# Expert stage: hots and masks in PSUM ring A, half 1's choice earlier in each engine's order, two bias rows issued as a couple

## The reference, cut to what matters

```python
xf = layernorm(x)                              # 1024 x 512
logits = xf @ router_w                         # 1024 x 8
gate_vals, idx = top_k(logits, 2)
gates = softmax(gate_vals)
for e in range(8):
    h = relu(xf @ w1[e] + b1[e]) @ w2[e] + b2[e]
    y = layernorm(xf + h, gamma[e], beta[e])
    out = out + sum(where(idx == e, gates, 0))[:, None] * y
x = x + out
```

## Time and profile before

| | us |
|---|---|
| median of 3 runs | 1158.26 |
| the 3 runs | 1157.27, 1158.26, 1162.53 |
| the profiled execution | 1157.11 |
| its span, first to last instruction | 1155.3 |

### The profile page before, as it was taken

One profiled execution on the slowest core, in us unless ns is written; L12 is line 12 of the kernel. 1 busy time (PEld: TensorE's weight loads), 2 busy tenths in 40 slices (PEclk: granted clock), 3 DMA queues, 4 the chain that ended last, 5 costly groups with the idle time before them and its releaser, 6 DMA issues.

```text
span 1155.3 us, 16126 instructions
## 1 busy us (share of the span) xinstructions
PE 1083.4 (94%) x5992; PEld 881.8 (76%) x5992; DVE 707.9 (61%) x1530; ACT 366.2 (32%) x671; POOL 149.1 (13%) x141
## 2 busy tenths in 40 slices
PE   3999799999999999999898999999999999999986
PEld 2777699888777777776898977777778888777653
DVE  7576777479676567457665479764653117723667
ACT  4234466525321211136566325221300011001132
POOL 4230202000000000300202000000000705000036
PEclk8999999999999999999999999999999999999897
DMA  6230101002312112000101004211337201100001
GB/s 210 84 117 1 38 2 38 1 5 92 90 48 64 56 47 78 1 1 1 38 1 38 1 5 130 72 46 55 108 148 246 74 1 37 35 1 1 1 18 55
DMA packets 34654, 60.16 MB, mean 52 GB/s; under 512 B 19440, under 2 KB 20400, under 8 KB 33936
## 3 DMA queue, kind: packets, MB, share of 16 engines
q1 hardware_dynamic: 12688, 41.21, 10.9%
q10 hardware_dynamic: 21888, 17.87, 4.8%
HBM read 48.59 MB, written 10.49 MB: 51 GB/s over the span
## 4 chain that ended last, share of the span: by engine, by line
PE 79%; DVE 11%; ACT 4%; issue 4%; POOL 1%; DMA 0%; ACTq 0%; POOLq 0%; DVEq 0%
PE ps_a L528 10%; PE ps_a L530 10%; PE ps_a L529 10%; PE ps_v L528 10%; PE ps_v L529 9%; PE ps_v L530 9%; PE ps_a L885 5%; PE ps_v L725 4%; PE ps_v L736 3%; PE ps_a L549 2%; PE ps_a L660 2%; DVE expk L1532 2%; ACT work L1063 1%; DVE qmax L1626 1%; PE ps_v L614 1%
## 5 line engine op out<-in xcount | busy, mean ns | idle before, releaser
L528 PE MATMUL ps_a<-ht_hi,w_hi 128*128 128x512 f32 x488 | 193.8, 397 | 2.7 <-DVE w_lo L1798 0.9
L530 PE MATMUL ps_a<-ht_hi,w_lo 128*128 128x512 f32 x488 | 191.6, 393 | 0.0
L529 PE MATMUL ps_a<-ht_lo,w_hi 128*128 128x512 f32 x488 | 191.3, 392 | 0.0
L974 ACT ACTIVATE work<-ps_a,col_sb 128x512 f32<-128x512 f32 x96 | 66.7, 719 | 203.0 <-PE ps_a L530 144.7
L528 PEld LDWEIGHTS ps_a<-ht_hi,w_hi 128*128 128x128 f32 x488 | 92.5, 189 | 26.0 <-DVE headmask_r L1497 1.3
L1651 DVE TENSOR_TENSOR xm<-ps_v,xm 128x512 f32<-128x512 f32 x80 | 55.2, 690 | 86.0 <-PE ps_v L530 85.5
L530 PEld LDWEIGHTS ps_a<-ht_hi,w_lo 128*128 128x128 f32 x488 | 92.3, 189 | 19.9
L529 PEld LDWEIGHTS ps_a<-ht_lo,w_hi 128*128 128x128 f32 x488 | 92.4, 189 | 19.4
L528 PE MATMUL ps_v<-w_hi,f_hi 128*128 128x512 f32 x256 | 101.7, 397 | 0.0
L528 PE MATMUL ps_v<-w_hi,ht_hi 128*128 128x512 f32 x224 | 92.0, 411 | 9.7 <-issue 5.8
L530 PE MATMUL ps_v<-w_hi,f_lo 128*128 128x512 f32 x256 | 99.7, 389 | 0.0
(11 more groups left out here) (238 smaller groups left out, 1964.9 us busy)
## 6 DMA issues: line engine op xcount, KB each, us to landing
stage<-wstream SPq DMA_DIRECT2D x62, 512.0 KB, 3.7
adj_d<-adj_win ACTq DMA_DIRECT2D x16, 256.0 KB, 2.9
adj<-adj_d ACTq DMA_DIRECT2D x2, 2048.0 KB, 12.3
xt_d<-xt_hi SPq DMA_DIRECT2D x2, 1024.0 KB, 5.0
xt_d<-xt_lo SPq DMA_DIRECT2D x1, 2048.0 KB, 11.4
ht_hi<-xt_d ACTq DMA_DIRECT2D x1, 2048.0 KB, 7.7
ht_lo<-xt_d ACTq DMA_DIRECT2D x1, 2048.0 KB, 12.4
x_again<-x ACTq DMA_DIRECT2D x8, 256.0 KB, 9.3
```

The lines of the kernel that those rows point to most:

```text
L528: nc.tensor.matmul(ps, left[0], right[0], start=first, stop=False)
L529: nc.tensor.matmul(ps, left[0], right[1], start=False, stop=False)
L530: return nc.tensor.matmul(ps, left[1], right[0], start=False, stop=last)
L974: nc.scalar.activation(work[:, n % 4, :], psA[:, i % BANKS, :], func, **how).then_inc(a_empty, 1)
```

## The change

It does three things, none of which changes what is computed.

First, the transposed hots and the four masks of each half are written to ring A, between the hidden layer and the next input's transposes; ring V has only products, logits and `z`, and the scales of tile 0. The scales of tile 1, which were in ring V, go to ring A.

Second, the orders: on PE `route(1)` stands behind tile 1 rather than tile 2, scales 0, the logits' transposes and both hidden products of half 1 follow it directly, and tile 2 comes behind them with `turn_hots(1)` in its middle. Scales 1 move behind tile 3, and from tile 5 on a tile is issued with the scales of two tiles before. On DVE `choose(1)` and `low_hidden(1)` come ahead of tile 2's additions, the four multiplications of `mask_hidden` are two pairs with an addition between, and `take_scales` follows with one or two tiles' delay. On ACT the copies of half 1's input come ahead of the squares of tile 0, and its logits, gates, hidden layer and hots ahead of the squares of tile 2.

Third, `second_bias(t)` issues the two 16-row matmuls of a tile one behind the other, on rows 0 to 15 and 32 to 47, ahead of both sixes (they open the sums in PSUM); before, each closed its own six.

```diff
 TAIL_A = numbered(
...
     + [("hidden", 0, m) for m in range(2)]
+    + [("hot", 0)] + masks(0)
     + [("turn", 1, k) for k in range(KT)]
...
             def turn_hots(h):
                 pe.wait_ge(hots_ready, h + 1)
-                ps = tail_bank("hot", h)
+                ps = bank_a(TA + TAIL_A["hot", h])
...
+            def second_bias(t):
+                for q in range(2):
+                    nc.tensor.matmul(tail_bank("z", q, t), hotT[rows_of(q), nodes(t)], small_r[rows_of(q), 0, :], start=True,
+                                     stop=False)
 
             def second_layer(q, t):
                 h = t // HALF_NT
-                taken_v(pe, "mask", q, 1, h)
-                ps = tail_bank("z", q, t)
+                taken_a(pe, "mask", q, 1, h)
+                ps = psV[:, (TV + TAIL_V["z", q, t]) % BANKS, :]
                 for m in range(2):
...
-                nc.tensor.matmul(ps, hotT[rows_of(q), nodes(t)], small_r[rows_of(q), 0, :], start=False,
-                                 stop=True).then_inc(v_full, 1)
+                last.then_inc(v_full, 1)
...
             pe.wait_ge(w2_ready, 1)
+            second_bias(0)
             second_layer(0, 0)
             second_layer(1, 0)
+            second_bias(1)
             second_layer(0, 1)
             turn_experts_input(1)
             second_layer(1, 1)
+            route(1)
             pick_scales(0)
+            turn_logits(1)
+            hidden(1, 0)
+            hidden(1, 1)
+            second_bias(2)
             second_layer(0, 2)
+            turn_hots(1)
             second_layer(1, 2)
-            route(1)
-            hidden(1, 0)
-            turn_logits(1)
-            hidden(1, 1)
-            pick_scales(1)
+            spread_hots(1)
+            second_bias(3)
...
+            for t in range(HALF_NT + 1, NT):
+                second_bias(t)
+                pick_scales(t - 2)
                 second_layer(0, t)
+                if t == NT - 1:
+                    pick_scales(NT - 2)
                 second_layer(1, t)
...
             take_hots(0)
+            high_turned(1)
             square(0)
-            high_turned(1)
+            take_logits(1)
             square(1)
-            square(2)
-            take_logits(1)
+            raise_gates(1)
             take_hidden(1, 0)
-            raise_gates(1)
             take_hidden(1, 1)
-            square(3)
             take_hots(1)
-            for t in range(HALF_NT, NT):
+            for t in range(2, NT):
                 square(t)
```

More of the change, by code:

```diff
@@ L220 @@
     + [("hidden", 1, m) for m in range(2)]
-    + [name for t in range(2, NT) for name in scales(t)]
+    + [("hot", 1)] + masks(1)
+    + [name for t in range(1, NT) for name in scales(t)]
 )
 TAIL_V = numbered(
-    [("lin", t) for t in range(4)] + [("logits", 0), ("lin", 4), ("hot", 0), ("lin", 5)] + masks(0)
-    + [("lin", 6), ("lin", 7)]
-    + both_z(0) + both_z(1) + scales(0) + both_z(2) + [("logits", 1)] + scales(1) + both_z(3)
-    + [("hot", 1)] + masks(1)
-    + [name for t in range(4, NT) for name in both_z(t)]
+    [("lin", t) for t in range(4)] + [("logits", 0)] + [("lin", t) for t in range(4, NT)]
+    + both_z(0) + both_z(1) + scales(0) + [("logits", 1)]
+    + [name for t in range(2, NT) for name in both_z(t)]
 )
@@ L1180, in take_hots @@
             def take_hots(h):
-                i = TV + TAIL_V["hot", h]
-                act.wait_ge(v_full, i + 1)
-                act.wait_ge(v_empty, done(i - 1))
-                nc.scalar.activation(hotT[:, half(h)], psV[0:3 * SET, i % BANKS, :], ACT.Copy).then_inc(v_empty, 1)
+                i = TA + TAIL_A["hot", h]
+                act.wait_ge(a_full, i + 1)
+                nc.scalar.activation(hotT[:, half(h)], psA[0:3 * SET, i % BANKS, :], ACT.Copy).then_inc(a_empty, 1)
             def take_hidden(h, m):
@@ L1886, in low_hidden, with mask_hidden @@
                                             ALU.subtract).then_inc(h1_split, 1)
-            def mask_hidden(h):
-                dve.wait_ge(h1_split, 2 * h + 2)
-                taken_a(dve, "hidden", h, 1)
-                for _, q, m, _ in masks(h):
+            def mask_hidden(h, q):
+                if q == 0:
+                    dve.wait_ge(h1_split, 2 * h + 2)
+                    taken_a(dve, "hot", h)
+                for m in range(2):
+                    i = TA + TAIL_A["mask", q, m, h]
+                    dve.wait_ge(a_full, i + 1)
                     nc.vector.tensor_tensor(hm[q][h][:, m, :, :],
-                                            tail_job("mask", q, m, h).unsqueeze(1).to_broadcast([P, 2, 512]),
-                                            h1[:, m, h, :, :].bitcast(f32), ALU.mult).then_inc(v_empty, 1)
+                                            psA[:, i % BANKS, :].unsqueeze(1).to_broadcast([P, 2, 512]),
+                                            h1[:, m, h, :, :].bitcast(f32), ALU.mult).then_inc(a_empty, 1)
             def add_z(q, t):
@@ L1950, in _ @@
             take_scales(0)
+            choose(1)
+            low_hidden(1)
             add_z(0, 2)
+            mask_hidden(1, 0)
             add_z(1, 2)
-            choose(1)
-            take_scales(1)
-            low_hidden(1)
+            mask_hidden(1, 1)
             add_z(0, 3)
             add_z(1, 3)
-            mask_hidden(1)
+            take_scales(1)
+            add_z(0, 4)
             take_scales(2)
-            for t in range(HALF_NT, NT - 1):
+            add_z(1, 4)
+            for t in range(HALF_NT + 1, NT - 1):
+                take_scales(t - 2)
                 add_z(0, t)
                 add_z(1, t)
-                take_scales(t - 1)
+            take_scales(NT - 3)
             last = NT - 1
```

27 lines of the change are left out of this document (12 added, 15 removed).

## The result

The changed kernel takes 1146.04 us (median of 4 runs, 1144.35 to 1147.17) against 1157.76 for the kernel before in the same comparison: a ratio of 0.9894, 95% interval 0.9857 to 0.9931. Over all executions of this study it is 12.5 us: 1147.2 on average for 20 of the changed kernel, 1159.7 for 113 of the kernel before.

What follows compares the result with a forecast made beforehand. PE, whose two stalls delay half 1's masks, then POOL's late rounds, bound the kernel. Steps 1 to 4 gain 7.8 us, less 1.2 for half clock: 1158.26 - 6.6 = 1151.7 us, ratio 0.994, range 1149.0 to 1155.5.

Steps and rivals of the forecast that it cites:

- Steps 1 to 4: From the ring change through half 1's input and masks to POOL's late rounds: end 7.8 us earlier at full clock.
- new wait at the transposes: PE, now early, waits 1.0 to 1.4 us at the transposes of half 1's input for the normalised tiles.
- Step 5: At the transposes of half 1's input: PE's new wait is followed by 3.4 us of half clock, costing 1.2 us.
- rival (a): No fall of the clock at the new wait: the full 7.8 us gained, 1150.5 us; chance 0.25.
- Three of five waits of this length: PE waits of 1.3 to 2.0 us before 1080 us: three followed by half clock, taken as making the fall likelier.
- I carry the difference over: Sum made on the profiled execution, 1157.11 us; the median's 1.15 above it was assumed unchanged, giving 1158.26 - 6.6.
- steps 2 and 3: Step 2: half 1's input to route(1), 9.9 us earlier; step 3: route to masks, DVE's first multiplication 12.9 us earlier.
- Rivals (b) to (e): End, chance: (b) long half-clock 1153.7, 0.15; (c) slower POOL 1154.2, 0.10; (d) lasting half-clock 1162.5, 0.05; (e) split couple 1152.7, 0.05.
- half clock behind the masks: Sign against the forecast: half clock behind half 1's masks that holds the late tiles up.
- The rule on DVE and GpSimd: choose(1) on DVE, beside POOL's first two additions, could end up to 2.6 us later; sum 0 to 0.2 us later.

Runs made afterwards that it cites:

- the couples alone: The kernel before with only the bias rows changed, two issued together to open both sums of a tile: 1155.4 us, ratio 0.9958 to before.
- the scales in ring A: The changed kernel with tile 1's scales taken ahead of half 1's masks, in the masks' ring: 1143.0 us, ratio 0.9843 to before.
- the version with both: The changed kernel with tile 1's scales early in ring A and epsilon added on ACT instead of POOL: 1143.2 and 1141.5 us, ratios 0.986 and 0.9861 to before.

## Why the prediction was wrong: the clock of an execution that was not seen

**Steps 1 to 4 held.** By the prediction's own points, with 0.67 us added to the times of after:

| | predicted | found |
|---|---|---|
| statistics of tile 7 end | 1089.75 | 1089.50 |
| half 1's input normalised | 1093.2 | 1092.99 |
| new wait at the transposes | 1.0 to 1.4 | 1.43 |
| `route(1)` | 1097.1 | 1096.90 |
| masks on PE | 1110.1 | 1109.48 |
| DVE's first multiplication | 1110.7 | 1110.10 |
| `take_scales(1)` ends | 1119.2 | 1118.43 |
| a round of POOL | 4.04 | 4.11 |
| DVE's last end | 1143.85 | 1143.35 |

Each lies within 0.8 us. The sum of the four steps was 7.8 and is 8.3 in the profiles. Of the 13.5 us gained at DVE's first multiplication 5.2 are thus lost behind it, and three experiments show that POOL's late start and pace are what takes them: shorter additions, an earlier start and a shorter round each bring 2.8 to 3.6 us, the last two together 5.4, while the couples bring none at full clock.

**Step 5 failed, the clock, and in both directions.** First, the term of 1.2 us for a fall behind the new wait: there was none in eleven profiles, so rival (a) was the case at that place. "Three of five waits of this length" was a count over other places of the kernel in one execution, where other work runs ahead of the wait. The places differ, and one place differs between executions: the wait of 1.50 us at 514.52, followed by half clock there, is followed by it in 13 of the 20 profiles of all kernels and by none in 7, at 1.50 to 1.56 us in each. So the length of the wait alone doesn't tell. The half clock did come behind waits of 0.43 us and less, in two of the four profiles of after.

Second, and larger in the executions that have it, the stall that the change removes was priced by the one execution at hand. The 6.83 us of half clock behind it were taken as what it costs ("no half clock in this run outlived 7 us of work"). In two of four profiles of before it is 13.65, and the stage 3.4 us longer. So the same change is worth 8.2 us of stage against the one case and 11.6 against the other.

**A term was missing.** The sum ended with DVE's last instruction and carried the stretch behind it over; it is 1.09 us shorter, and what differs there is when the last packet of code is fetched, which the order of the work doesn't show.

**The account.** In the two profiles that were compared it closes: the 6.6 us of the forecast, 1.2 for the fall that didn't come, 0.5 in steps 1 to 4, 1.09 behind DVE's last end and 0.67 ahead of the stage, in code that is the same, are the 10.0 us between the spans. With the fall left out and the 1.09 put in, the forecast would have been 1149.4, still within the range; with the 0.5 and the 0.67 it would have been 1148.2, just below. The last 2.2 us down to 1146.04 lie in the step "I carry the difference over": the profile of before lies 1.15 us below the median that the prediction started from, that of after 1.13 above its own. The longer case of before fits this, as it raises the median and was not in the profile.

Over more executions: 8.2 or 11.6, and 1.1, is 9.3 to 12.7 us, where 11.7 to 12.5 were measured. With two of the four profiles in either case, the mean is 11.0; the 1.5 us left to the mean over the executions are open, since how often before has the longer case can't be counted without a profile of each, and the places of half clock ahead of the stage, up to 30.7 us of it in one profile and 6.8 in another, differ between executions more than that. Over 109 of the executions of before (those of the later comparisons), 1 us more of half clock goes with 0.34 us more time. By their mean granted clocks they have 49.6 us of half clock on average and the 20 of after 30.1: 19.5 apart, where the four profiles of each have 14.0 from the start of the stage on. If the part ahead of the stage is alike in both, which isn't shown, before has its longer case more often than in two of four.

**The range** went wrong with it. Its lower end, 1149.0, was the sum at full clock and 1.5 us for steps 2 and 3; it had no room for a dearer stall in before, although its three runs went from 1157.3 to 1162.5. **Rivals (b) to (e)** didn't happen (no fall at the new wait, POOL's late additions at 1.26 to 1.30 us, a couple of 0.50), and half clock behind the masks, listed as what would prove the forecast wrong, does happen and costs nothing, since it lies under POOL's pace.

The rule on DVE and GpSimd was told for two inputs in SBUF: `choose(1)` up to 2.6 us later. It took 1.6 us longer, by the two instructions shown above, and it lay on no path. The Trainium skill, "SBUF — State Buffer" (Who interferes with whom), says that the two engines exclude each other for whole instructions, with two inputs in SBUF and also in the two-port modes of a cast. The trace agrees: the cast and the second of the two comparisons end as POOL's additions end, and the three instructions are 0.18 and 0.36 us long without them. The prediction read its nearest row as "both slow down a little"; but `low_hidden(1)`, 2.38 us there beside POOL's addition, takes 1.28 in after at 1106.03, where POOL is idle, so that row had shown a hold-up of 1.1 us.

## What to carry to other kernels

A stall ahead of a busy TensorE can have a price that varies from one execution to the next (here by 3.4 us): price what is removed by several profiles, or let the range reach from the shortest half clock to one twice as long. Find the engine that will set the pace afterwards, and look there for the next gain: here 0.22 us of POOL's work in a round, moved to an idle ACT, brought 2.8 us, and an earlier start of its queue 3.1. In a ring of four banks, count four places back from every result that is moved.

## What the runs showed of the hardware

- **Half clock came in pieces** of 3.41, 6.83, 13.65 or 17.07 us in all profiles while PE had work. A wait of 1.43 us ahead of transposes was followed by none in eleven profiles, one of 3.02 us at the same place by 3.41 in one, three waits of 0.15 to 0.43 us in a row by 6.83 in three of eight, and one of 2.64 us by 6.83 or 13.65.
- **A packet of code beside the last store** goes with a store that lands in 3.2 us instead of 2.2. It goes by the kernel, not by the execution: all four profiles of before, the couples alone and the scales in ring A have it at 1.9 us behind DVE's end, and the version with both at 1.8; all four of after and the other kernels have it at 3.6 to 3.7. Why the end of the span then comes 1.09 us later, when the store's packets end only 0.5 later, stays open, and no kernel was made to move the packet alone.
- **POOL held up short DVE instructions until its own addition ended**: 0.18 became 0.68 us, 0.36 (two instructions) became 1.46, while the searches beside the same addition were not held up.
